# Layer-norm terms taken inside the stages, four blocks at a time, in place of two passes over all blocks

## What is computed

```
h  = tokenize(x)              # tanh scores, softmax over windows of 4 rows (stride 2), weighted rows, a projection
h  = h + attention(norm(h))   # 8 heads, three partial attentions over thirds of a head, a projection
h  = h + experts(norm(h))     # 4 experts, routed to one per row
norm(h) = (h - mean(h)) / sqrt(var(h) + 1e-5)      # over the 192 columns of a row
```

## Time and profile before

| | us |
|---|---|
| median of 3 runs | 2015.51 |
| lowest and highest run | 2015.36, 2016.34 |
| the profiled execution | 2016.56 |
| its span | 2014.8 |

### The profile page before, as it was taken

One profiled execution on the slowest core, in us unless ns is written; L12 is line 12 of the kernel. 1 busy time (PEld: TensorE's weight loads), 2 busy tenths in 40 slices (PEclk: granted clock), 3 DMA queues, 4 the chain that ended last, 5 costly groups with the idle time before them and its releaser, 6 DMA issues. The chain is left out here.

```text
span 2014.8 us, 58856 instructions
## 1 busy us (share of the span) xinstructions
PE 1813.5 (90%) x20032; PEld 1012.2 (50%) x20032; DVE 1483.6 (74%) x3647; ACT 1472.7 (73%) x2978; POOL 1304.8 (65%) x2326
## 2 busy tenths in 40 slices
PE   1888889828999999999999999999981999999998
PEld 1565656603444444444444444444430666666666
DVE  3666666737999999999999999999961555545454
ACT  1666666507899998999989999899971676766665
POOL 2666666566777777777777777777737655656561
PEclk9999999958999999999999999999995999999999
DMA  5434343114444444444444444444430223232322
GB/s 139 105 83 104 83 103 84 42 22 77 86 89 88 87 91 89 90 88 89 88 88 90 88 86 90 88 91 88 88 56 19 59 63 73 55 73 58 69 66 53
DMA packets 504063, 159.64 MB, mean 79 GB/s; under 512 B 452176, under 2 KB 503248, under 8 KB 504016
## 3 DMA queue, kind: packets, MB, share of 16 engines
q1 hardware_dynamic: 504016, 159.04, 37.2%
HBM read 37.41 MB, written 12.48 MB: 25 GB/s over the span
## 5 line engine op out<-in xcount | busy, mean ns | idle before, releaser
L716 DVE TENSOR_REDUCE tops<-p_maxa 128x6 f32<-128x762 f32 x512 | 482.8, 943 | 66.3 <-PE p_maxa L558 63.0
L629 PE MATMUL p_o<-probs,vn 127*32 127x256 f32 x6144 | 410.9, 385 | 0.2 <-DVE att L744 0.2
L554 PE MATMUL p_s<-qm,kt 32*128 32x256 f16 x3072 | 402.4, 276 | 1.8 <-DMA qm<-qk 0.8
L670 ACT ACTIVATE probs<-p_s 128x512 f32<-128x512 f32 x512 | 305.5, 597 | 111.6 <-PE p_s L554 98.0
L718 DVE TENSOR_REDUCE tops<-p_maxb 128x4 f32<-128x508 f32 x512 | 346.0, 676 | 0.0
L676 ACT ACTIVATE probs<-p_s 128x512 f32<-128x512 f32 x512 | 308.6, 603 | 0.0
L990 DVE TENSOR_TENSOR gel_lo<-gel,gel_hi 128x512 f16<-128x512 f32 x192 | 147.3, 767 | 217.1 <-ACT gel_hi L980 216.0
L673 ACT ACTIVATE probs<-p_s 128x512 f32<-128x512 f32 x512 | 304.2, 594 | 0.3 <-PE p_s L554 0.2
L558 PE MATMUL p_maxa<-kt,qt 24*128 24x256 f16 (+1 forms) x2048 | 283.3, 250 | 17.5 <-issue 8.7
L767 POOL TENSOR_TENSOR qk<-raw,one 128x384 f16<-128x384 f32 x128 | 105.7, 826 | 223.2 <-ACT raw L692 223.2
L972 ACT ACTIVATE gel<-f_w,b 128x512 f32<-128x512 f32 x192 | 131.9, 687 | 144.3 <-PE f_w L923 144.3
(11 more groups left out here) (200 smaller groups left out, 4576.6 us busy)
## 6 DMA issues: line engine op xcount, KB each, us to landing
xt_a<-in_xt SPq DMA_DIRECT2D x32, 512.0 KB, 4.3
xt_b<-in_xt SPq DMA_DIRECT2D x64, 256.0 KB, 5.2
out<-out_sb SPq DMA_DIRECT2D x32, 336.0 KB, 2.7
xt<-hx SPq DMA_TRANSPOSE x128, 2.3
kt<-qk SPq DMA_TRANSPOSE x128, 2.7
qt<-qk SPq DMA_TRANSPOSE x128, 2.5
qm<-qk SPq DMA_TRANSPOSE x128, 2.7
yt<-ay SPq DMA_TRANSPOSE x128, 2.3
```

The source lines that it names most:

```text
L554: return nc.tensor.matmul(o, kt[full(j), r, kind, g, :], qm[full(j), r % 2, versions, g, :], start=True, stop=True, skip_group_check=True)
L629: last = nc.tensor.matmul(p_o[32 * j:32 * j + 32, blocks, :], vn[0:NP, r, src:src + 32], probs[0:NP, r % 2, QUAD * g + j, kind * 256:(kind ...
L670: nc.scalar.activation(probs[:, r % 2, h + 1, 0:512], p_s[1][:, :, :].rearrange("p x n -> p (x n)"), ACT.Exp, scale=SCALE).then_inc(act_e1 ...
L716: nc.vector.tensor_reduce(top[:, q, pair, 4:10], p_ma[:, 0:6, 0:NP], AX.X, ALU.max, negate=True).then_inc(dve_ma[u], 1)
```

## The change

`norm_terms` and its two calls go. The first stage and the attention stage make `t.rstd` and `t.shift` themselves, for four blocks at a time.

In the first stage bn_stats go to a ring of two groups. In the round after, DVE does the three sums behind the softmax's weights at k = 1, the square, the scaling and the addition behind `weight_up` at k = 2, and behind the scores of k = 3 it waits for POOL's power, copies `rstd` and makes `shift`. POOL takes the power of 128 x 4 numbers at k = 2, between `diag` and `xa_lo`, when DVE's third step is done.

In the attention stage DVE turns each bn_stats into mean and variance with bn_aggr (L738), behind the second pair of maxima, and three waits move or come in. POOL adds epsilon and negates the mean of four blocks at the end of its body r = 2 (`moved_on`), and in body r = 3, between `hx` and the halves of `qk`, it takes the power and makes `rstd` and `shift` (`terms`, with one extra product into `spare`). Two memsets are added at the stage's start. Eleven bodies stand ahead of the loop in place of seven, and the last body is i = 131 in place of 130; four bodies fewer run in the loop.

```diff
--- before.py
+++ after.py
@@ first stage, DVE
+            def terms(i, par, step):
+                g = i - 3
...
+                st = stats[:, 1 - par]
+                if step == 1:
+                    dve.wait_ge(dve_stats, seen((i - 2) * G))
...
+                    nc.vector.tensor_tensor(mean[:, :], st[:, :, 1], st[:, :, 4], ALU.add)
+                    nc.vector.tensor_tensor(gap[:, :], st[:, :, 1], st[:, :, 4], ALU.subtract)
+                    nc.vector.tensor_tensor(var[:, :], st[:, :, 2], st[:, :, 5], ALU.add).then_inc(dve_norm, 1)
+                elif step == 2:
+                    dve.wait_ge(dve_norm, seen((i - 2) * 4 - 3))
+                    nc.vector.tensor_tensor(gap[:, :], gap[:, :], gap[:, :], ALU.mult)
+                    nc.vector.tensor_scalar(var[:, :], var[:, :], 1.0 / C, EPS, ALU.mult, ALU.add).then_inc(dve_norm, 1)
+                    dve.wait_ge(dve_norm, seen((i - 2) * 4 - 2))
+                    nc.vector.scalar_tensor_tensor(out=var[:, :], in0=gap[:, :], scalar=0.25, in1=var[:, :],
+                                                   op0=ALU.mult, op1=ALU.add).then_inc(dve_norm, 1)
+                elif step == 3:
+                    dve.wait_ge(pool_root, seen(i - 2))
+                    nc.vector.tensor_copy(t.rstd[:, bass.ds(g * G, G)], root[:, :])
+                    nc.vector.scalar_tensor_tensor(out=t.shift[:, bass.ds(g * G, G)], in0=mean[:, :], scalar=-0.5, in1=root[:, :],
+                                                   op0=ALU.mult, op1=ALU.mult).then_inc(dve_norm, 1)
...
                     softmax(i, 1 - par, k)
+                    terms(i, par, k)
                     u = n - 2 * G - 1
...
@@ first stage, POOL, between diag and xa_lo
+                    if k == 2 and within(i - 3, NG):
+                        pool.wait_ge(dve_norm, seen((i - 2) * 4 - 1))
+                        nc.gpsimd.tensor_tensor(root[:, :], var[:, :], t.half[:, :], ALU.pow).then_inc(pool_root, 1)
...
-def norm_terms(nc, t, NB, name):
...
@@ attend
-            for i in range(-4, 3):
+            for i in range(-4, 7):
...
@@ attend, DVE
             def body(i, r):
+                if within(i - 3, NB):
+                    dve.wait_ge(dve_h, seen(i - 2))
+                    dve.wait_ge(dve_aggr, seen(i - 3))
                 maxima(i, r, 0)
                 if within(i - 3, NB):
-                    dve.wait_ge(dve_h, seen(i - 2))
-                    nc.vector.bn_stats(t.stats[:, bass.ds((i - 3) * 6, 6)], t.h[:, bass.ds((i - 3) * C, C)])
+                    nc.vector.bn_stats(stats[:, :], t.h[:, bass.ds((i - 3) * C, C)]).then_inc(dve_stats, 1)
+                    dve.wait_ge(dve_stats, seen(i - 2))
+                    if r == 3:
+                        dve.wait_ge(pool_norm, seen(i - 5))
                 maxima(i, r, 1)
+                if within(i - 3, NB):
+                    nc.vector.bn_aggr(moments[:, (r + 1) % U, :], stats[:, :]).then_inc(dve_aggr, 1)
...
@@ attend, POOL
+            def moved_on(i, r):
+                if r == 2 and within(i - 3, NB):
+                    pool.wait_ge(dve_aggr, seen(i - 2))
+                    pool.wait_ge(pool_norm, seen(i - 6))
+                    nc.gpsimd.tensor_tensor(varied[:, :], moments[:, :, 1], eps[:, :], ALU.add).then_inc(pool_norm, 1)
+                    nc.gpsimd.tensor_tensor(neg[:, :], moments[:, :, 0], minus[:, :], ALU.mult).then_inc(pool_norm, 1)
+            def terms(i, r):
+                if r == 3 and within(i - 4, NB):
+                    pool.wait_ge(pool_norm, seen(i - 5))
+                    nc.gpsimd.tensor_tensor(root[:, :], varied[:, :], t.half[:, :], ALU.pow).then_inc(pool_norm, 1)
+                    pool.wait_ge(pool_norm, seen(i - 4))
+                    nc.gpsimd.tensor_tensor(spare[:, :], root[:, :], one[:, :].broadcast_to([128, U]), ALU.mult)
+                    nc.gpsimd.tensor_tensor(t.rstd[:, bass.ds(i - 7, U)], root[:, :], one[:, :].broadcast_to([128, U]), ALU.mult)
+                    nc.gpsimd.tensor_tensor(t.shift[:, bass.ds(i - 7, U)], neg[:, :], root[:, :], ALU.mult).then_inc(pool_norm, 1)
```

More of the change, by code:

```diff
@@ L187, in tokenize @@
         act_z, pe_h, act_h = sem("act_z"), sem("pe_h"), sem("act_h")
-        dve_stats = sem("dve_stats")
         act_split, pool_split = sem("act_split"), sem("pool_split")
+        stats = sb("stats", [128, 2, G, 6])
+        mean, gap, var, root = (sb(x, [128, G]) for x in ("mean", "gap", "var", "root"))
+        dve_stats, dve_norm, pool_root = sem("dve_stats"), sem("dve_norm"), sem("pool_root")
         block = ctx.enter_context(nc.Block())
@@ L352, in body @@
                     softmax(i, 1 - par, k)
+                    terms(i, par, k)
                     u = n - 2 * G - 1
                     if within(u, NB):
+                        q, kk = (par, k - 1) if k else (1 - par, G - 1)
                         dve.wait_ge(act_h, seen(u + 1))
-                        nc.vector.bn_stats(t.stats[:, bass.ds(u * 6, 6)], t.h[:, bass.ds(u * C, C)]).then_inc(dve_stats, 1)
+                        nc.vector.bn_stats(stats[:, q, kk, :], t.h[:, bass.ds(u * C, C)]).then_inc(dve_stats, 1)
             loop(dve, body)
@@ L447, in attend @@
         one = sb("one", [128, 1])
+        stats, moments = sb("att_stats", [128, 6]), sb("moments", [128, U, 2])
+        varied, root, spare, neg = (sb(x, [128, U]) for x in ("varied", "att_root", "spare", "negated"))
+        eps, minus = sb("eps", [128, U]), sb("minus", [128, U])
         ones16 = sb("ones16", [128, 128], F16)
@@ L478, in attend @@
         pe_proj, dve_h = sem("pe_proj"), sem("dve_h")
+        dve_stats, dve_aggr, pool_norm = sem("att_dve_stats"), sem("dve_aggr"), sem("pool_norm")
         block = ctx.enter_context(nc.Block())
         def loop(eng, body):
-            for i in range(-4, 3):
+            for i in range(-4, 7):
                 body(i, i % U)
-            rounds = (NB - 7) // U
+            rounds = (NB - 11) // U
             with eng.Fori(0, rounds) as j:
                 for r in range(U):
-                    body(j * U + (3 + r), (3 + r) % U)
-            for i in range(3 + U * rounds, NB + 3):
+                    body(j * U + (7 + r), (7 + r) % U)
+            for i in range(7 + U * rounds, NB + 4):
                 body(i, i % U)
```

13 lines of the change are left out of this document (9 added, 4 removed).

## The result

The changed kernel takes 2057.41 us (median of 4 runs, 2055.48 to 2059.41), the kernel before 2015.43 (4 runs, 2013.78 to 2016.34): 42 us more, a ratio of 1.0209 with a 95% interval of 1.0192 to 1.0227. The forecast was 2038 us, in a range of 2012 to 2060. So the change is slower, as forecast, and costs nearly twice what the sum said.

A forecast was written before the change was run, and what follows sets the result against it. It saw two boundary holes where only POOL's power runs, and stages with little room for moved work. Boundaries -40.3, first stage +37.8, attention +21, straight-line code +4 sum to +22.5 us: 2038 us predicted, range 2012 to 2060.

The forecast's parts named there:

- The boundaries: Between the stages: removing the two 128-column powers was to save 19.1 us at the first and 21.2 at the second, -40.3 together.
- the tail: First stage's four last rounds, whose chain runs through the same engines: forecast to lose 0.45 us each, 1.8 us.
- The power of four columns: POOL's new small power in the first stage: forecast at 0.83 us, at least 0.18 and at most 1.5.
- the line between the two rows: Estimate from POOL's one-column operation (0.18 us) and 128-column power (20.80): 0.161 us a column, so 0.83 for four.
- `xa_lo` late by 1.0: First stage, each round: POOL's power and its wait for DVE's step 2 were to start `xa_lo` 0.95 to 1.1 us late.
- The collision of the moments: First stage, each round: DVE's moments were to sit until POOL's `diag` ends, delaying `band` by 0.35 us, between 0 and 0.5.
- TensorE's clock "stays as it is": Claim that TensorE's granted clock would not change, since it still stops several us in the boundary holes; no cost in the sum.
- The attention stage: DVE's added waits were to cost 0.7 us per four bodies, 30 times: +21 us, between +5 and +36.
- the price of a body without the wait for POOL: Attention stage: 0.1 us per body for DVE's waits; one body of four also waits 0.3 us for POOL's negated means.
- Straight-line code: Four more attention bodies outside the loop, at 9.13 us against 8.13 inside: +4 us, at least 0 and at most 5.
- the power did not fit into POOL's gap at k = 2: Rival: first stage's step 2 and power delay `xa_lo` by only 0.2 us, giving 2006 us, faster; chance 0.12.
- both pay more: Rival: power costs 1.5 us or POOL's fourth-body work meets DVE's minima; first stage near 52, attention near 30, 2061 us; chance 0.15.

## Why the prediction was right, and where it was too small

- *The boundaries*, -40.3: -38.5 measured. At the second, -21.2 was right within 0.3. At the first the small operations and the power behind the last bn_stats took 2.2 us where 2.4 was allowed (they are eight operations, not seven), but from the last `weight_up` to the end of that bn_stats it is 8.65 us in place of 5.39: the tail lost 3.3 us and not 1.8.
- *The power of four columns*, 0.83 us from the line between the two rows: 1.01. The bounds held it. The 0.18 us of a one-column copy, taken for the fixed part, was too little.
- *`xa_lo` late by 1.0*: 1.10. *The collision of the moments*, 0.35: one of the three sits for `diag` as forecast, except in the half-clock rounds, and the rounds hold 0.30 beyond the lateness; that the collision is all of the 0.30 is likely and not shown. A round grows by 1.40 where the sum had 1.35, and 28 x 1.40 = 39 against 37.8.
- *TensorE's clock "stays as it is"*: this is the step that failed. It was looked at in the boundaries alone. A round that is late leaves TensorE idle for 1.5 to 1.7 us where it had 0.29, and in nine rounds it then ran at 1.2 GHz for some 3 us: 9 x 1.37 = 12.3 us that no term of the sum held. With it the first stage's +51.5 is accounted for.
- *The attention stage*, 0.7 us per four bodies and +21: 1.0 per four bodies, and 24.2 us that go when the waits move. The mechanism was right: bn_stats' wait was forecast to cost the third maximum 0.12 us, and it starts 0.11 later. The mis-sized term is the price of a body without the wait for POOL: 0.1 was allowed, and the three took 0.26, 0.16 and 0.15 more. The fourth, with 0.4 allowed, took 0.43 more; its third maximum starts 0.47 later. bn_aggr, of which the prediction said only that it is queued behind, costs nothing that shows.
- *Straight-line code*, +4: +5.2 when done alone. That the size held is luck, because the earlier trace rows were misread. The loop starts at body 3, and the two `att` at 472.44 and 508.97 are those of bodies 1 and 5: three of the four bodies that were timed as straight-line code belong to the loop's first pass. Straight-line bodies cost 0.1 to 0.3 us each; the first pass costs more, wherever it starts.
- The rivals: the power did not fit into POOL's gap at k = 2, but it does fit into the one at k = 0, and then the first stage's price is nearly gone. The rival "both pay more" came nearest (2061), with other reasons than the two it named.

The sum with what was measured in place of the forecast: -38.5 + 39 + 12.3 + 24.2 + 5.2 = +42. Its last term is a median whose cause is open, and smaller than the scatter of the attention piece. That the time still lies in the range, 3 us below its upper end, owes something to luck: the range let single terms go to their bounds, and not the clock, which was put at nothing.

## What to carry to other kernels

A hole of 40 us at two boundaries is cheaper than a quarter of a us in each of 127 bodies and 1.4 us in each of 28 rounds: multiply before moving work out of a hole into a tight loop, and ask first what makes the hole long. When work goes into a gap of an idle engine, what counts is when its input is ready and how far that is ahead of the next instruction that others wait for, not the length of the gap; the same power made a round's `xa_lo` 1.1 us late at one place, and at another the round grew by 0.08 us in all. And a wait belongs on the latest instruction that still protects the data: moving four waits by one instruction gave 24 us.

## What the runs showed of the hardware that was not expected

- TensorE's clock falls inside a stage that keeps it busy for four fifths of the time: after 1.70 us of idle ahead of one matmul group, 0.51 of full speed was granted in 3.3 us that began 0.9 us behind that group's start. Unneeded matmuls in that gap took it away and saved 7 us.
- POOL's power costs 20.8 us for 128 columns and 1.01 for four, which by the line between the two makes 0.16 us a column and 0.37 fixed; a product of four columns takes 0.20 and is no measure for it.
- A loop with the attention code unchanged ran at 32.43 to 32.68 us for four bodies in different kernels, with the same number of its minima beside POOL's work; why is open. The first pass through it took some 36 us, also where it began eight bodies later.
